# Counting the degrees of the nodes: from the pass for the maximum to the scatter of rows

## The reference

```python
# layer 0: messages from dst's features and edge features, summed by src
aggregated = jax.ops.segment_sum(messages, src, num_segments=n)
# layer 1: attention; a maximum, a sum of exponents and a weighted sum by dst
m = jax.ops.segment_max(e, dst, num_segments=N)
# layer 2: degree by destination (with loops added once more)
deg = jax.ops.segment_sum(jnp.ones_like(col), col, num_segments=n)
dinv = jnp.where(deg > 0, jax.lax.rsqrt(deg), 0.0)
# layer 3: mean over incoming edges
agg = agg / jnp.maximum(deg, 1.0)[:, None]
```

## Time and profile before

| | |
|---|---|
| median of 3 runs | 4012.09 us (4009.74 to 4016.07) |
| profiled execution, its own time | 4007.71 us |
| its span, first to last instruction | 4006.0 us |
| mean granted clock of TensorE | 0.84 |
| TensorE busy | 2767.3 us, 69% |
| VectorE busy | 2620.8 us, 65% |
| GpSimd busy | 1983.2 us, 50% |
| ScalarE busy | 1608.0 us, 40% |

### The profile page before, as it was taken

One profiled execution on the slowest core, in us unless ns is written; L12 is line 12 of the kernel. 1 busy time (PEld: TensorE's weight loads), 2 busy tenths in 40 slices (PEclk: granted clock), 3 DMA queues, 4 the chain that ended last, 5 costly groups with the idle time before them and its releaser, 6 DMA issues. The chain is left out here.

```text
span 4006.0 us, 89562 instructions
## 1 busy us (share of the span) xinstructions
PE 2767.3 (69%) x19674; PEld 2009.0 (50%) x19675; DVE 2620.8 (65%) x7923; ACT 1608.0 (40%) x4084; POOL 1983.2 (50%) x2354
## 2 busy tenths in 40 slices
PE   2314554455454555888888888888888967769599
PEld 2213333333333334787777877787785222234345
DVE  8724555555555554888888888888886759950501
ACT  1001222222222223776777777776775613320201
POOL 0015666566666666777777777777772000000100
PEclk9955556666666657999999999999999979979797
DMA  9971222221222223777777777777774848848082
GB/s 387 415 291 59 65 65 63 64 62 61 64 64 65 65 64 106 205 203 202 204 204 203 202 206 202 202 205 197 202 206 171 294 173 295 296 151 325 22 325 100
DMA packets 702415, 696.60 MB, mean 174 GB/s; under 512 B 51182, under 2 KB 633536, under 8 KB 692640
## 3 DMA queue, kind: packets, MB, share of 16 engines
q1 hardware_dynamic: 672706, 637.13, 50.5%
q0 software_dynamic: 25792, 54.52, 4.0%
q10 hardware_dynamic: 3870, 4.37, 0.3%
HBM read 340.91 MB, written 354.90 MB: 174 GB/s over the span
## 5 line engine op out<-in xcount | busy, mean ns | idle before, releaser
L885 POOL DMA_INDIRECT sorted_rows<-rows,posi x806 | 779.8, 967 | 577.1 <-issue 246.4
L836 PE MATMUL s_peq<-sb_w1bb,eT 128*128 128x256 f32 x806 | 395.5, 591 | 584.9 <-ACT eT L703 359.6
L1166 DVE SCALAR_TENSOR_TENSOR acc<-acc,keep,pm 128x256 f32<-128x256 f32 x1504 | 717.4, 477 | 76.3 <-DVE acc L1166 36.3
L997 POOL TENSOR_SCALAR ohs_e<-iota,rt 128x128 f32<-128x128 f32 x1128 | 669.6, 608 | 11.4 <-DMA rt<-sorted_rows 11.4
L1093 PE MATMUL pm<-ohw_e,ohs_e 128*128 128x128 f32 x3008 | 662.7, 302 | 0.0
L1006 POOL TENSOR_TENSOR hid<-pre_e,excess 128x512 f32<-128x512 f32 x376 | 498.7, 1326 | 313.5 <-ACT excess L1033 313.5
L836 PEld LDWEIGHTS s_peq<-sb_w1bb,eT 128*128 128x128 f32 x806 | 188.9, 288 | 635.3 <-ACT eT L703 398.7
L1099 PE MATMUL px<-PN,dT 128*128 x4512 | 498.5, 219 | 0.2 <-ACT dT L1040 0.2
L1049 ACT ACTIVATE ohw_e<-ohd_e,rt 128x128 f32<-128x128 bf16 x1504 | 474.6, 386 | 0.0
L1092 PE MATMUL pm<-ohd_e,ohs_e 128*128 128x128 bf16 x1504 | 334.3, 222 | 198.1 <-DVE acc L1166 182.8
L1093 PEld LDWEIGHTS pm<-ohw_e,ohs_e 128*128 128x128 f32 x3008 | 459.7, 193 | 0.0
(11 more groups left out here) (299 smaller groups left out, 4469.3 us busy)
## 6 DMA issues: line engine op xcount, KB each, us to landing
count_matrices<-acc SPq DMA_DIRECT2D x1504, 128.0 KB, 2.0
ab<-count_matrices SPq DMA_DIRECT2D x75, 1600.0 KB, 7.8
sorted_rows<-zrow SPq DMA_DIRECT2D x188, 528.0 KB, 9.9
rt<-sorted_rows SPq DMA_DIRECT2D x376, 264.0 KB, 3.0
arb<-count_matrices SPq DMA_DIRECT2D x25, 1664.0 KB, 6.8
arb<-count_matrices SPq DMA_DIRECT2D x25, 1536.0 KB, 6.4
ef<-in_edge_attr_dram SPq DMA_DIRECT2D x60, 364.0 KB
sorted_rows<-rows,posi POOLq DMA_INDIRECT x806
```

The lines of the kernel that those rows point to most:

```text
L836: nc.tensor.matmul(pe_q[:, q % 2, 0:2 * D], eT[:, q % 2, :], w1bb[:], start=True, stop=True).then_inc(s_q, 1)
L885: pool.indirect_dma_start(sortd, bass.IndirectOffsetOnAxis(ap=posi[:, h, c:c + 1], axis=0), rows[:, h, c, :], None).then_inc(s_sc[h], 16)
L997: last = nc.gpsimd.tensor_scalar(ohs[:, k, j, :], iota128[:], rt[:, k, j, D + 1:D + 2], None, ALU.is_equal)
L1166: nc.vector.scalar_tensor_tensor(acc[:, k % 2, j, :], before, keep[:, at:at + 1] if isinstance(at, int) else keep[:, ds(at, 1)], pm[:, j / ...
```

## The change

In the scatter, VectorE's `begin` makes a third one-hot, ohL, of the destination's place in its tile: 13 x 128 columns for each half, between ohD and `base`. TensorE's `lookups` gets 13 matmuls ahead of the look-ups, one for each column: ohL as the stationary operand (128 columns) and ohD as the moving one (25 columns), added up in the 25 columns of lk behind the look-ups. They give the count, for each node, of the half's edges. VectorE's `places` adds them to DEG, which is cleared at the start. From the pass for the maximum the matmuls, their wait on SyncE and the copies to DG are taken away, and from the block behind it the 25 products and the copy to DEG.

```diff
@@ -590,6 +590,7 @@
                 posi = sb2("posi", [P, 2, CH], I32)
                 ohF = sb2("ohF", [P, 2, CH, QP], F16)
                 ohD = sb2("ohD", [P, 2, CH, NT], F16)
+                ohL = sb2("ohL", [P, 2, CH, P], F16)
                 ohT = sb2("ohT", [P, 2, 4, P])
                 base = sb2("base", [P, 2, 4, 4, NT])
                 junkW = sb2("junkW", [P, CH, NREL])
@@ -735,6 +736,8 @@
                                                 tile[:, 1, c].unsqueeze(2).to_broadcast([P, CH, QP]), ALU.is_equal)
                         nc.vector.tensor_tensor(ohD[:, h, :, :], iota25[:].unsqueeze(1).to_broadcast([P, CH, NT]),
                                                 tile[:, 0, c].unsqueeze(2).to_broadcast([P, CH, NT]), ALU.is_equal)
+                        nc.vector.tensor_tensor(ohL[:, h, :, :], iota128[:].unsqueeze(1).to_broadcast([P, CH, P]),
+                                                lo[:, 0, c].unsqueeze(2).to_broadcast([P, CH, P]), ALU.is_equal)
                         for j in range(4):
                             b = slice(QP * j, QP * j + QP)
                             last = nc.vector.tensor_tensor(base[b, h, :, j, :], runs[b, ds(n, 1), :].rearrange("p a (q d) -> p (a q) d", d=NT),
@@ -763,6 +766,7 @@
                             if c % 4 == 3 or c == CH - 1:
                                 last.then_inc(s_rk, 1)
                         dve.wait_ge(s_lk, n + 1)
+                        nc.vector.tensor_tensor(DEG[:], DEG[:], lk[:, CH * NT:(CH + 1) * NT], ALU.add)
                         nc.vector.tensor_tensor(junkL[:], lk[:, 0:CH * NT].rearrange("p (c d) -> p c d", d=NT), ohD[:, h, :, :],
                                                 ALU.mult).then_inc(s_lc, 1)
                         dve.wait_ge(s_lc, 3 * n + 1)
@@ -773,6 +777,7 @@
 
                     link = Chain(dve, s_bz)
                     link(nc.vector.memset(base[:], 0.0))
+                    link(nc.vector.memset(DEG[:], 0.0))
                     begin(0, 0, True)
                     places(0, 0)
                     begin(0, 1, True)
@@ -820,6 +825,9 @@
                             pe.wait_ge(s_ot, n + 1)
                             if not first:
                                 pe.wait_ge(s_lc, 3 * n - 2)
+                            for c in range(CH):
+                                nc.tensor.matmul(lk[:, CH * NT:(CH + 1) * NT], ohL[:, h, c, :], ohD[:, h, c, :],
+                                                 start=(c == 0), stop=(c == CH - 1), skip_group_check=True)
                         for q in PARTS[part]:
                             a, b = 4 * q, min(4 * q + 4, CH)
                             k = (b - a) * QP
@@ -1490,13 +1498,11 @@
 
             with ExitStack() as ctx:
                 un = ctx.enter_context(nc.sbuf_tensor("un", [P, NT, P], F32))
-                pg = ctx.enter_context(nc.psum_tensor("m_pg", [1, len(CUTS), BANK], F32))
                 MXv = MX[:].rearrange("p (q d) -> p q d", q=NT)
                 BIG = 1e30
                 s_ld = s_ab
                 s_un = sem("m_where_no_edge")
                 s_mx = sem("m_max")
-                s_dg = sem("m_degree")
                 s_ago = sem("m_act_passed")
                 block = ctx.enter_context(nc.Block())
 
@@ -1507,7 +1513,6 @@
                     with sp.Fori(1, NT // R) as i:
                         for r in range(R):
                             sp.wait_ge(s_un, ((i - 1) * R + r) * 2 + 2)
-                            sp.wait_ge(s_dg, ((i - 1) * R + r) * 2 + 2)
                             load(i * R + r, r)
 
                 @block.scalar
@@ -1539,25 +1544,6 @@
                     step(0, True)
                     with dve.Fori(1, NT) as s:
                         step(s, False)
-                    dve.wait_ge(s_dg, 2 * NT)
-                    for c, (a, b) in enumerate(CUTS):
-                        nc.vector.tensor_copy(DG[0:1, a:b], pg[:, c, 0:b - a])
-
-                @block.tensor
-                def _(pe):
-                    def step(i, first, final):
-                        for r in range(R):
-                            pe.wait_ge(s_ld[r], i * 16 + 16)
-                            for c, (a, b) in enumerate(CUTS):
-                                last = nc.tensor.matmul(pg[:, c, 0:b - a], ones[:, 0:1],
-                                                        ab[:, r, :, :].rearrange("p q d -> p (q d)")[:, a:b],
-                                                        start=first and r == 0, stop=final and r == R - 1,
-                                                        skip_group_check=True)
-                            last.then_inc(s_dg, 2)
-                    step(0, True, False)
-                    with pe.Fori(1, NT // R - 1) as i:
-                        step(i, False, False)
-                    step(NT // R - 1, False, True)
 
 
             blocks.close()
@@ -1568,11 +1554,9 @@
                 dm = ctx.enter_context(nc.sbuf_tensor("dm", [P, 2 * NT], F32))
                 dT = ctx.enter_context(nc.sbuf_tensor("dmT", [2 * NT, P], F32))
                 tp = ctx.enter_context(nc.psum_tensor("x_tp", [P, 2, BANK], F32))
-                pd = ctx.enter_context(nc.psum_tensor("x_pd", [P, BANK], F32))
                 pr = ctx.enter_context(nc.psum_tensor("x_pr", [2 * NT, BANK], F32))
                 s_t = sem("x_turned")
                 s_r = sem("x_reduced")
-                s_d = sem("x_degrees")
                 s_m = sem("x_rows")
                 s_mt = sem("x_rows_turned")
                 s_mc = sem("x_rows_copied")
@@ -1581,9 +1565,6 @@
 
                 @block.tensor
                 def _(pe):
-                    for t in range(NT):
-                        last = nc.tensor.matmul(pd[:, t:t + 1], DG[0:1, t * P:(t + 1) * P], ones[0:1, 0:1], start=True, stop=True)
-                    last.then_inc(s_d, 1)
                     for c, (a, b) in enumerate(CUTS):
                         if c >= 2:
                             pe.wait_ge(s_r, c - 1)
@@ -1596,8 +1577,6 @@
                 @block.vector
                 def _(dve):
                     link = Chain(dve, s_chain, chained)
-                    dve.wait_ge(s_d, 1)
-                    nc.vector.tensor_copy(DEG[:], pd[:, 0:NT])
                     for c, (a, b) in enumerate(CUTS):
                         dve.wait_ge(s_t, c + 1)
                         last = nc.vector.tensor_reduce(mc[:, 0, a // P:b // P],
```

## The result

On chips where the kernel before took 4011.09 us (median of 20 runs, 4001.14 to 4023.61), the changed kernel took 4021.07 us (20 runs, 4008.51 to 4031.88): ratio 1.0023, 95% interval 1.0012 to 1.0034. It is slower by 9 us, 5 to 14. Forecast were +26 us. The direction was right and the size was not: the term for ohL was too large, the one for the restarts was perhaps too small, and the one for the maximum pass was right.

The account below looks back on a forecast made before the run. Scatter: GpSimd's issuing plus a wait at each of 62 halves; maximum pass: TensorE. Terms 62 + 15 - 51 = +26 us on 4007.71 gave 4033.7, or 4038 as median; range 3970 to 4110.

Parts of the forecast that it names:

- ohL's stops, +62 us: Scatter: each ohL on VectorE stops GpSimd's DMAs, about 1.0 us a half paid, 62 us in all, bounds 13 and 117.
- GpSimd waits anyway for 238 of 1264 us, a fifth, so about 1.0 us a half is paid: Scatter: cut the 1.26 us stop by GpSimd's waiting share, giving 62 us where the whole stop would make 78.
- break-even of 0.82 us a half: Scatter's added cost per half at which the 51 us gained in the maximum pass is used up, 51 / 62.
- the DMA at 651.01: Scatter DMA started between two one-hots, 1.29 us against a 0.958 median, read as stopped for the running one-hot's rest.
- Later restarts, +15 us: Scatter: VectorE's added work puts posi 0.7 us later, delaying GpSimd's restarts 0.25 us a half, 15 us; bounds 0 and 223.
- rival (2): Scatter restarts wait for the added chain, 2.3 us a half, 4104 us; sign: waits over 330 us; chance 0.15.
- the crawl: Scatter: VectorE's small L745 instructions issue slowly within a half, ending 2.2 us after GpSimd's last DMA; cause unknown.
- what is left after GpSimd has stopped is done at 0.32 us a piece: Scatter: VectorE's leftover small instructions finish quickly once GpSimd stops, so posi is put only 0.7 us later.
- The maximum pass, -51 us: Maximum pass: without 350 matmuls VectorE bounds it, and the transposes start 51 us earlier; bounds 33 and 56.
- Rival (3): Loads bound the maximum pass, so only 33 us come back: +44, 4056 us; chance 0.08.
- rival (1): Scatter: GpSimd covers it, ohL's stops cost 13 us and restarts 0, so -38, 3974 us; chance 0.27.

Follow-up runs that it names:

- reduce_alone: Kernel before plus, in each half, one VectorE sum over 13 x 128 zeros (one SBUF input) in ohL's place: ratio 1.0009, scatter 1271.2 us.
- onehot_alone: Kernel before plus only the one-hot ohL in each half, degrees still counted in the maximum pass: ratio 1.0022, scatter 1274.3 us.
- products_alone: Kernel before plus, in each half, the 13 products against a cleared one-hot array and the addition to DEG: ratio 1.0052, scatter 1292.1 us.
- after_no_stop: Changed kernel with a one-input sum over zeros in place of making ohL, run under free issue: ratio to before 0.9867, scatter 1026.2 us.
- count_before_turn: Changed kernel with products moved ahead of the next half's turn and DEG's addition behind posi, free issue: ratio to before 1.0021, scatter 1087.5 us.
- after_again: Changed kernel run again, unaltered, under free issue: ratio to before 1.0022, scatter 1087.3 us.
- one_in_thirteen: Kernel before with 12 of the 13 indirect DMAs of each half left out, under slow issue: scatter 708 us.

## Why the prediction was wrong in size

**ohL's stops, +62 us.** The mechanism held: one DMA over 1400 ns in 40 of 62 halves (58 under free issue), and an equally long instruction with one input that doesn't stop. The step that failed is "GpSimd waits anyway for 238 of 1264 us, a fifth, so about 1.0 us a half is paid". In the changed kernel the DMAs are 41 us busier and not 62, so even if all of it is paid the term was 21 us too large: in 21 of 62 halves, a third, no DMA started while ohL ran, under free issue in 4. And alone nearly nothing is paid (51 us busier, 10 longer, of which a sum that stops nothing made 7). My reading, which no run tests, is that a wait of GpSimd there ends with something that the others do sooner while GpSimd stands still, so that a stop gives them the time that the wait would have given. A share of idle time isn't a chance of being covered. Against the break-even of 0.82 us a half, ohL by itself cost 0.16.

The stop itself was put at 1.26 us a half and measured 1.05 under free issue, 65 us. That this is near the 62 is luck, since a fifth had been taken off for waits that GpSimd doesn't have there. The reading of the DMA at 651.01 was half right: by the 0.83 us it was stopped by ohF, the one-hot that ran when it started (to 651.48, and it ended at 652.30), and not by ohD. The rule of the Trainium skill (SBUF — State Buffer, section "SBUF: two separate sides"), an exclusive lock of a VectorE instruction with two SBUF inputs against a GpSimd instruction that reads SBUF, agrees with reduce_alone against onehot_alone: 1362 against 2630 ns at most.

**Later restarts, +15 us.** Open in size, between 12 and 43 us. By the parts it was too small: products_alone cost 28 us, and with ohL the scatter grew by 53, so 43 beside ohL's own 10, of which 15 are explained by no part alone. By the changed kernel's own trace the 53 are 41 us of longer DMAs and 12 of longer gaps. Whether the stops, covered when ohL stands alone, are paid when the products are there too would show in after_no_stop under slow issue, and there is no such run. What is shown is where the forecast went past the mechanism. The size of the work was overstated (1.5 us for the products, 0.38 measured), and 28 us were paid for it all the same. The waits didn't move to posi, as forecast, but into the half, most of them ahead of the ninth DMA; the prediction's sign for rival (2), waits over 330 us, didn't come (240.3). What grew is VectorE's wait for the look-ups, from 169 to 381 us in all. The junkW group, expected deeper in the crawl, is out of it: none of its 744 steps is over 0.5 us. The step "what is left after GpSimd has stopped is done at 0.32 us a piece" passed over that semaphores, too, are often only seen then; the earlier trace rows held a trace of it (ScalarE's rows at 933.72 begin just with posi at 933.48).

**The maximum pass, -51 us.** Right: -53.8, with 95.5 us from first maximum to transposes (95 to 100 forecast) and 0.3 us behind it. Rival (3), the loads, is out.

**The sum.** 77 - 51 was forecast, 53 - 54 was measured in the traces, and +9 (5 to 14) by the medians; the 10 us between are within what the unchanged stages vary by from trace to trace, and no experiment ties them to the change. By the parts, rival (1) had the stops' small price right and the restarts' wrong, and rival (2) is what the excess over ohL looks like, at 0.7 us a half in place of 2.3. Under free issue no restart waits, so the sum is the measured stops alone: 65 - 54 = +11, and 1.0022 of 3787 is +8.

## What to carry to other kernels

A stop of an engine is paid in full where its own work sets the pace (65 of 65 us here); where it waits, ask what ends its waits, and whether the stop lets that happen sooner. A VectorE instruction with two SBUF inputs beside GpSimd's indirect DMAs is best cut into pieces shorter than their pitch: at the same place, 36 us of stops fell to 18. With the move, which took 65 to 36 by where the DMAs happened to start, it turned a loss of 8 us into a gain of 39. Where a loop's period is more than any engine's own work (20.4 us, with 16.4 on GpSimd and 11.4 on the rest), find out what couples them before changing it.

## What the runs showed of the hardware

The same program had two paces of issue. Under slow issue, in the kernel before, SyncE's three loads of a half leave 2.0 and 2.9 us apart. VectorE's pairs of junkW (an instruction and the reading of its accumulator), otherwise 0.25 us, take up to 2.1 in these rows, since one instruction comes 0.7 us after the other, or twice that:

```profile
918.56 0.32 SPq L639 DMA_DIRECT2D ef<-in_edge_attr_dram  x1
920.60 0.02 SPq L640 DMA_DIRECT2D ef<-in_edge_attr_dram  x1
923.49 0.02 SPq L644 DMA_DIRECT2D ef<-in_edge_attr_dram  x1
```

```profile
924.25 0.08 DVE L745 DVE_READ_ACCUMULATOR junkW<-iotar,typc,relt 128x1 f32 x1 [0.41 <-issue]
924.98 0.32 DVE L745 SCALAR_TENSOR_TENSOR junkW<-iotar,typc,relt 128x100 f32<-128x100 f32 x1 [0.66 <-issue]
926.40 0.08 DVE L745 DVE_READ_ACCUMULATOR junkW<-iotar,typc,relt 128x1 f32 x1 [1.09 <-issue]
927.12 0.32 DVE L745 SCALAR_TENSOR_TENSOR junkW<-iotar,typc,relt 128x100 f32<-128x100 f32 x1 [0.64 <-issue]
```

Under free issue (count_before_turn) they are 0.5 us apart with GpSimd issuing all the time:

```profile
813.99 0.32 SPq L641 DMA_DIRECT2D ef<-in_edge_attr_dram  x1
814.50 0.33 SPq L642 DMA_DIRECT2D ef<-in_edge_attr_dram  x1
815.02 0.23 SPq L646 DMA_DIRECT2D ef<-in_edge_attr_dram  x1
```

It builds up with the length of a run of DMAs. In the kernel before, counted over the scatter, 50 of 405 steps from one instruction of junkW to the next took over 0.5 us beside GpSimd's first eight DMAs after a pause, 27 of 94 beside the ninth and tenth, and all 76 from the eleventh on. In the changed kernel all are beside the first eight or in a pause, and none is that long. Slow issue is worth 240 us of 4020, and no property of a chip, since chip 10 was in both.

The two conditions also differ in what the trace holds. A DMA of the scatter reports its completion 16 times, 12896 times in all. The trace of the kernel before has 2161 of these events and the other full scatters under slow issue 2221 to 5125; after_again has all 12896, and no trace under free issue lacks more than 82. one_in_thirteen, at a time of slow issue, has all of its 992, and none of junkW's late steps. The page of a profile gives the landing time of a line only where none is missing (the first line is the kernel before, the second after_again).

```profile
sorted_rows<-rows,posi POOLq DMA_INDIRECT x806
```

```profile
sorted_rows<-rows,posi POOLq DMA_INDIRECT x806, 2.3
```

That would fit the writing of event records as the coupling: too many events for it while GpSimd issues in a row, and engines that are held up with it. The Trainium skill (NOTIFIC — the notification-queue block, section "7.1 Overflow: three behaviours, one of which stalls the engine") has it that a full record path can hold its engine back. But missing events and late engines may also be two effects of a third thing. No run here tests that, and the cause stays open; so it is also open whether an execution without a profile has slow issue at all.
